# Layer 0 of a graph network on one core: where the gather loop waits for landings

## The chip, the cores and the metric

One Trainium2 chip, one of its NeuronCores. The time is the device time of one launch in microseconds (us); of three runs of the kernel before, the median is 8332.26 us (8326.56 to 8350.35). Engines are called PE (TensorE), DVE (VectorE), ACT (ScalarE), POOL (GpSimd) and SP (SyncE).

## The reference

There are 12,500 nodes of 16 features and 412,500 directed edges, sorted by destination. Each of two layers works on the normalised, rectified node features. The first layer is the one that matters here:

```
h = relu(edge_attr_16 @ W1 + b1)              # 256 values per edge
w_edge = (h @ W2 + b2).reshape(-1, 16, 16)    # a 16x16 matrix per edge
msgs = einsum('ei,eio->eo', x[src], w_edge)   # gathered source row times its matrix
aggr = segment_sum(msgs, dst)
out  = relu(batchnorm(aggr + x @ root + bias)); x = x + out
```

The second layer makes messages from `edge_attr_8` and again sums them by node. All is computed in float32, or in split parts that come to it.

## The kernel before

The kernel runs in stages, each with its own semaphores: `setup`, `layer0`, `between`, `layer1`, `finish`. The change is in `layer0` (L710 to L1155), which fills some 60 to 5036 us of the profiled execution.

`layer0` walks 404 groups of 1024 edges. A group is 128 partitions by T = 8 tiles. Every engine runs the same list of groups through `each_ring`, a loop whose body is four groups (buffers `r` = 0 to 3), and all order between engines is by counting semaphores.

- SP loads the edge features `ea` of a group (L779), 64 KB, two buffers.
- POOL, function `gather` (L795 to L807), fetches the source rows. For each tile it issues one indirect DMA that reads 128 rows of 128 bytes from the HBM table `gather_rows` into `xg[r][:, t, :]`. The row numbers are in `idx[r]`. There are 8 such gathers for a group, and 7 when `r` is 3 (from the second lap on), where PE and DVE make the eighth tile from a table in SBUF (`gather_dense`, `pick_rows`): 3132 in all. Before a group POOL waits for `idx_ready` and for the group four earlier to be done with the buffer. Before gather t, from the third on, it waits until gather t-2 of the same group has landed, and then adds one to `gathers_begun`. No instruction waits for `gathers_begun`.
- ACT, `body` (L872): two pairs of relus (`relu`, L842, from PSUM `ps_h` to `hT`), the copy `eT` (L836), then `indices` (L817), which writes `idx` three groups ahead (`AHEAD` = 3), then the splitting of edge features and messages.
- PE, `body` (L950 on): `hidden` (L906, two products into `ps_h`), `edge_weights` (L920, 16 instructions for half a group into four banks `ps_w`), `hidden`, `edge_weights`, `turn` (L896, transposes the features of the group two ahead), `gather_dense` in one group of four (L948), and `scatter` (L934, the sum by destination of the group before). `hidden` is written again only when ACT has read it, and it reads `eT`.
- DVE: `unit` (L1003) multiplies a bank `ps_w` with two tiles of `xg`; this is where a gathered row is first needed. `sum_unit` (L1010) adds up, `add_bias` (L1016) ends with `msg_ready`. Then follow the one-hot matrices (L1034) and the split of the messages.

After the last group's load SP also clears the tables that the second layer adds into (L595, L596).

Of the kernel before, what the change touches and what calls it, by code (L numbers as in the profile page):

```python
# [28 lines left out]
T = 8  # L29
# [22 lines left out]
def need(engine, sem, count):  # L52

    if isinstance(count, int) and count <= 0:
        return
    engine.wait_ge(sem, count)  # L56
# [15 lines left out]
def each_ring(engine, count, body, ring=4, laps=1):  # L72


    for c in range(laps * ring):
        body(c, c % ring, c // ring)
    assert count % ring == 0
    with engine.Fori(0, count // ring - laps - 1) as i:
        for u in range(ring):
            body(i * ring + (laps * ring + u), u, i + laps)  # L80
    for u in range(ring):
        c = count - ring + u
        body(c, u, c // ring)
# [626 lines left out]
def layer0(nc, S, k, sem, c, ea16, n_passes):  # L710
# [44 lines left out]
    xg_in = [[sem(f"xg_in{r}{t}") for t in range(T)] for r in range(RING)]  # L755
# [5 lines left out]
    def dense(r, lap):  # L761

        return r in DENSE and not (isinstance(lap, int) and lap == 0)
# [6 lines left out]
    with nc.Fori(0, n_passes) as _:  # L770
        with nc.Block() as block:

            @block.sync
            def _(sp):
                def load(g, r, lap):
                    s = r % 2
                    e0 = min(g * GE, S.E - GE) if isinstance(g, int) else sp.snap(g * GE)
                    need(sp, q["ea_used"], g - 1)
                    sp.dma_start(ea[s][:, :, :].rearrange("p t f -> p (t f)"),  # L779
                                 ea16[bass.ds(e0, GE), :].rearrange("(p t) f -> p (t f)", t=T)  # L780
                                 ).then_inc(ea_in[s], 16)
                    if dense(r, lap):
                        need(sp, q["col_free"], lap - 1)
                        sp.dma_start(col_b[:, :], k.col_rows[bass.ds(g, 1), :].broadcast_to([KP, P])
                                     ).then_inc(q["col_in"], 16)
                    if isinstance(g, int) and g == 1:
                        sp.dma_start(rows_in[:, :, :],
                                     k.rows[0:S.N, :].rearrange("(k p r) f -> p k (r f)", p=KP, r=KR)
                                     ).then_inc(q["node_in"], 16)
                each_ring(sp, G, load, RING, 2)  # L790
                clear_tables(sp, S, k, q["zeroed"])

            @block.gpsimd
            def _(pool):
                def gather(g, r, use):  # L795
                    pool.wait_ge(q["idx_ready"], g + 1)
                    need(pool, q["msg_ready"], g - RING + 1)
                    pool.sem_inc(q["gathers_begun"], 1)
                    for t in range(T - 1 if dense(r, use) else T):
                        if t >= 2:  # L800
                            pool.wait_ge(xg_in[r][t - 2], 16 * (use + 1))
                            pool.sem_inc(q["gathers_begun"], 1)
                        pool.indirect_dma_start(  # L803
                            xg[r][:, t, :], None, k.rows,
                            bass.IndirectOffsetOnAxis(ap=idx[r][:, t:t + 1], axis=0)
                        ).then_inc(xg_in[r][t], 16)
                each_ring(pool, G, gather, RING)  # L807

                pool.wait_ge(q["msg_ready"], G)
                pool.dma_reset()  # L810
# [1206 lines left out]
```

## Time and profile before

| what | us |
|---|---|
| median of three runs | 8332.26 |
| the profiled execution | 8296.17 |
| its span, first to last instruction | 8294.4 |
| `layer0`, from the first gather to the start of the next stage, about | 4976 |
| one group of it, 4976 / 404 | 12.3 |

The profiled execution is one run with the hardware profiler on; its span leaves out what lies before the first and after the last instruction, 1.8 us. A busy share over the whole span mixes the stages, which have different limits. "Idle before" is the time in which an engine did nothing ahead of an instruction, put down to the semaphore event that came last; "issue" means that no such event was seen just before, and "remote" that a semaphore moved for which the profile shows no source close enough in time. Ends of PE's instructions are modelled.

### The profile page before, as it was taken

The page shows a single profiled execution, that of the slowest core. Times are in us where ns is not written, and L with a number is a line of the kernel's source. Part 1 is how long each engine was busy: PE and PEld are TensorE (multiplying, and loading weights), DVE is VectorE, ACT ScalarE, POOL GpSimd, SP SyncE. Part 2 cuts the span into 40 slices and gives each one's busy share as a digit, 9 for nine tenths or more (in the row PEclk, how much of TensorE's full clock was granted, in tenths as well). Part 3 has the DMA queues.
Part 4 walks back from the last instruction along what each step waited for, and adds up shares of the span by engine and source line. Part 5 has one row for each costly group of instructions (what it writes and reads, how often), then busy time and mean ns, then how long its engine had stood idle before and what let it go on. Part 6 is the DMA issues. An engine that isn't in the chain of part 4 may idle for free. (4 is left out here: it accounts for less than half of the span.)

```text
span 8294.4 us, 193483 instructions
## 1 busy us (share of the span) xinstructions
PE 7333.8 (88%) x52997; PEld 6345.0 (76%) x52997; DVE 6680.6 (81%) x17449; ACT 4443.1 (54%) x8279; POOL 5653.6 (68%) x4866
## 2 busy tenths in 40 slices
PE   6888887888888888888888886999999999999998
PEld 5666666666666666666666665999999999999996
DVE  6667776777677777777777767999999999999997
ACT  4333343333333333333333434888888877778884
POOL 5656665666566666665666664888888888888886
PEclk8999999999999999999999998999999999999999
DMA  2111111111111111111111114445555555555544
GB/s 59 17 17 17 17 17 16 17 17 17 17 17 17 17 17 17 17 17 17 17 17 17 17 17 100 75 73 75 75 73 75 73 73 73 72 73 74 75 73 65
DMA packets 713464, 341.73 MB, mean 41 GB/s; under 512 B 422115, under 2 KB 656599, under 8 KB 713427
## 3 DMA queue, kind: packets, MB, share of 16 engines
q0 software_dynamic: 332928, 64.86, 13.5%
q1 hardware_dynamic: 379313, 272.94, 13.3%
q10 hardware_dynamic: 1186, 3.51, 0.1%
q8 instruction: 15, 0.25, 0.0%
q14 instruction: 22, 0.18, 0.0%
HBM read 307.85 MB, written 32.96 MB: 41 GB/s over the span
## 5 line engine op out<-in xcount | busy, mean ns | idle before, releaser
L803 POOL DMA_INDIRECT xg<-gather_rows,idx x3132 | 3001.6, 958 | 1996.5 <-issue 1259.3
L920 PE MATMUL ps_w<-W2s,hT 128*128 128x256 f32 x12928 | 3244.2, 406 | 63.0 <-issue 33.9
L920 PEld LDWEIGHTS ps_w<-W2s,hT 128*128 128x128 f32 x12928 | 2632.5, 205 | 627.7 <-issue 126.7
L1746 POOL DMA_INDIRECT sums<-total,row x1616 | 2548.8, 1577 | 541.8 <-issue 487.7
L1709 PE MATMUL ps_wide<-hot_col,placed 128*128 128x392 f32 x12928 | 2436.4, 345 | 9.1 <-DVE placed L1545 3.2
L1709 PEld LDWEIGHTS ps_wide<-hot_col,placed 128*128 128x128 f32 x12928 | 2315.3, 196 | 19.1 <-issue 12.8
L842 ACT ACTIVATE hT<-ps_h,b1c 128x512 f32<-128x512 f32 x1616 | 1024.7, 680 | 2288.5 <-remote 1662.2
L1003 DVE TENSOR_TENSOR prod<-ps_w,xg 128x512 f32<-128x512 f32 x1616 | 1082.2, 689 | 326.2 <-issue 66.1
L906 PE MATMUL ps_h<-eT,W1p 96*128 96x512 bf16 x1616 | 526.8, 407 | 656.3 <-ACT eT L836 480.1
L1644 ACT ACTIVATE square<-iota_col,minus_col 128x784 bf16<-128x784 int16 x1212 | 1061.2, 938 | 74.1 <-issue 57.6
L1545 DVE SCALAR_TENSOR_TENSOR placed<-ps_r,src_r,halves 128x512 fp32r<-128x512 f32 x1616 | 1099.1, 746 | 0.1
L1010 DVE TENSOR_REDUCE msg<-prod 128x32 f32<-128x512 f32 x1616 | 1059.6, 677 | 0.0
L1650 ACT ACTIVATE hot_col<-square,ones 128x2352 fp32r<-128x2352 bf16 x404 | 910.5, 2254 | 0.0
L1034 DVE TENSOR_SCALAR hot<-iota,rel_t 128x256 bf16<-128x256 bf16 x3232 | 737.8, 303 | 116.0 <-DVE ea_res L983 80.8
L983 DVE TENSOR_TENSOR ea_res<-ea,ea_parts 128x128 f32<-128x128 f32 x404 | 117.7, 291 | 858.3 <-ACT ea_parts L823 512.2
L906 PEld LDWEIGHTS ps_h<-eT,W1p 96*128 96x128 bf16 x1616 | 137.0, 97 | 811.5 <-issue 769.9
L1683 PE MATMUL ps_q<-q_win,hotT 128*128 128x128 bf16 x9696 | 609.6, 219 | 18.7 <-DVE hotT L1484 18.7
L1502 DVE TENSOR_TENSOR prod<-ps_q,e 128x512 f32<-128x512 f32 x808 | 553.9, 686 | 42.9 <-issue 40.8
L1683 PEld LDWEIGHTS ps_q<-q_win,hotT 128*128 128x128 bf16 x9696 | 548.1, 98 | 19.8 <-DVE hotT L1484 19.8
L1511 DVE TENSOR_REDUCE pre<-prod 128x64 f32<-128x512 f32 x808 | 550.7, 682 | 0.1
L852 ACT ACTIVATE parts<-msg_res 128x128 bf16<-128x128 f32 x404 | 125.0, 309 | 592.9 <-DVE msg_res L1022 428.9
L836 ACT ACTIVATE eT<-ps_e 96x1024 bf16<-96x1024 bf16 x404 | 408.9, 1012 | 1.9 <-PE ps_e L896 1.9
(229 smaller groups left out, 5613.6 us busy)
## 6 DMA issues: line engine op xcount, KB each, us to landing
dst_row<-dst_rows SPq DMA_DIRECT2D x404, 256.0 KB
src_row<-src_rows SPq DMA_DIRECT2D x404, 128.0 KB
xg<-gather_rows,idx POOLq DMA_INDIRECT x3132, 2.4
q_win<-q_rows SPq DMA_DIRECT2D x404, 96.0 KB
ea<-in_edge_attr SPq DMA_DIRECT2D x404, 64.0 KB
sums<-total,row POOLq DMA_INDIRECT x1616
e<-in_edge_attr SPq DMA_DIRECT2D x404, 32.0 KB
q_rows<-Q SPq DMA_DIRECT2D x12, 768.0 KB, 5.1
```

Source lines behind the costliest of these rows:

```text
L803: pool.indirect_dma_start(xg[r][:, t, :], None, k.rows, bass.IndirectOffsetOnAxis(ap=idx[r][:, t:t + 1], axis=0)).then_inc(xg_in[r][t], 16)
L842: a.activation(hT[s][:, j, :], ps_h[j][:, :], ACT.Relu, bias=k.b1[:, j:j + 1]).then_inc(q["relued"], 1)
L920: last = pe.matmul(to, hT[half][:, j, col:col + P], k.W2[:, j, :], start=(j == 0), stop=(j == 1 and not with_b2))
L1003: v.tensor_tensor(prod[u % 2][:, :, :, :], ps_w[u][:, :, :, :], xg[r][:, 2 * u:2 * u + 2, 0:D].unsqueeze(2).broadcast_to([P, 2, D, D]), AL ...
L1010: v.tensor_reduce(msg[s][:, 2 * u:2 * u + 2, :], prod[u % 2][:, :, :, :], X, ALU.add).then_inc(q["reduced0"], 1)
L1034: last = v.tensor_scalar(hot[s][:, t, :], k.iota[:, :], k.rel[:, bass.ds(g, 1), t:t + 1].rearrange("p g t -> p (g t)"), None, ALU.is_equal)
L1545: last = v.scalar_tensor_tensor(placed[s][:, w, :, :, :].rearrange("p r f a -> p r (f a)"), ps_r[:, :, :], src_r[:, bass.ds(g, 1), w], hal ...
L1644: last = a.activation(square[:, n, :], iota_col[:, :], ACT.Square, bias=minus_col[:, bass.ds(g, 1), WIDE - ACT_TILES + n])
L1650: a.activation(hot_col[s][:, WIDE - ACT_TILES:, :, :].rearrange("p w a b -> p (w a b)"), square[:, :, :].rearrange("p w b -> p (w b)"), AC ...
L1683: last = pe.matmul(ps_q[u][:, w, :, :].rearrange("p h j -> p (h j)"), hotT[s][:, t * P:(t + 1) * P], q_win[s][:, part * P:(part + 1) * P], ...
L1709: last = pe.matmul(ps_wide[:, 2 * r + a, 0:S.LC], placed[s][:, w, r * HR:(r + 1) * HR, :, part].rearrange("p r f -> p (r f)"), hot_col[s][ ...
L1746: pool.indirect_dma_start(k.sums[t], bass.IndirectOffsetOnAxis(ap=row[r][:, t:t + 1], axis=0), total[r][:, t, :], None, compute_op=ALU.add ...
```

## The change

POOL's wait for a landing stands in front of one gather of a group only. The fifth gather (t = 4) waits for the landing of the second (t = 1). The third, fourth, sixth, seventh and eighth are issued without a wait. `gathers_begun` is raised twice for a group and not seven times. What each gather fetches, the buffers, their number and all waits of the other engines stay.

```diff
                     pool.sem_inc(q["gathers_begun"], 1)
                     for t in range(T - 1 if dense(r, use) else T):
-                        if t >= 2:
-                            pool.wait_ge(xg_in[r][t - 2], 16 * (use + 1))
+                        if t == T // 2:
+                            pool.wait_ge(xg_in[r][t - 3], 16 * (use + 1))
                             pool.sem_inc(q["gathers_begun"], 1)
                         pool.indirect_dma_start(
                             xg[r][:, t, :], None, k.rows,
```

## Rows read from the trace of the kernel before

**Rows 1.** the page: busy time of each engine over the span

```profile
PE 7333.8 (88%) x52997; PEld 6345.0 (76%) x52997; DVE 6680.6 (81%) x17449; ACT 4443.1 (54%) x8279; POOL 5653.6 (68%) x4866
```

**Rows 2.** busy time by stretch; columns: stretch, us, then each engine

```profile
60.00:5036.00 4976.00, 4158.91 (x25124) 3305.26 (x25124) 3565.38 (x9890) 1914.77 (x4039) 3000.57 (x3132) 0.93 0.11 18
95.00:285.00 190.00, 159.17 (x972) 125.69 (x969) 137.69 (x382) 76.42 (x157) 117.01 (x122) 0.95 0.11 18
4986.00:5010.00 24.00, 20.36 (x139) 16.06 (x138) 18.43 (x52) 10.67 (x23) 6.83 (x8) 1.00 0.36 123
5036.00:8000.00 2964.00, 2890.95 (x25879) 2800.78 (x25880) 2834.26 (x6925) 2336.81 (x3860) 2415.22 (x1542) 0.99 0.52 76
```

**Rows 3.** groups of the first layer, 60 to 5036 us: busy, mean ns, idle before

```profile
L803 POOL DMA_INDIRECT xg<-gather_rows,idx x3132 | 3001.6, 958 | 1996.5 <-issue 1259.3 <-DMA xg<-gather_rows,idx 621.1 <-ACT idx L817 115.2
...
L1003 DVE TENSOR_TENSOR prod<-ps_w,xg 128x512 f32<-128x512 f32 x1612 | 1079.6, 689 | 325.9 <-issue 66.1 <-remote 54.8 <-DMA xg<-gather_rows,idx 38.0
...
L842 ACT ACTIVATE hT<-ps_h,b1c 128x512 f32<-128x512 f32 x1616 | 1024.7, 680 | 2288.5 <-remote 1662.2 <-PE ps_h L906 486.8 <-issue 135.4
...
L906 PE MATMUL ps_h<-eT,W1p 96*128 96x512 bf16 x1616 | 526.8, 407 | 656.3 <-ACT eT L836 480.1 <-issue 166.5 <-ACT hT L842 7.2
```

**Rows 4.** timeline of POOL, 2499 to 2507 us: start, length, [idle before]

```profile
2500.12 0.94 POOL L803 DMA_INDIRECT xg<-gather_rows,idx  x1 [0.30 <-issue]
2501.37 0.94 POOL L803 DMA_INDIRECT xg<-gather_rows,idx  x1 [0.30 <-issue]
2503.27 0.94 POOL L803 DMA_INDIRECT xg<-gather_rows,idx  x1 [0.96 <-DMA xg<-gather_rows,idx]
2504.52 0.94 POOL L803 DMA_INDIRECT xg<-gather_rows,idx  x1 [0.30 <-issue]
2506.48 0.94 POOL L803 DMA_INDIRECT xg<-gather_rows,idx  x1 [1.01 <-issue]
```

**Rows 5.** DMA issues of the page: median us from issue to landing

```profile
xg<-gather_rows,idx POOLq DMA_INDIRECT x3132, 2.4
```

**Rows 6.** instructions on tile xg, start to 2500 us: how many of each

```profile
L803 POOL DMA_INDIRECT xg<-gather_rows,idx x1536: 938/943/3520, 61.9 to 2498.7; - x192
L1003 DVE TENSOR_TENSOR prod<-ps_w,xg x784: 678/692/693, 82.7 to 2494.6; 128x512 f32<-128x512 f32 x196
```

**Rows 7.** waits, 95 to 285 us: us in total, times, longest

```profile
DVE prod L1003 <- DMA xg<-gather_rows,idx: 36.7, 27, 2.2
```

**Rows 8.** timeline of PE, 2500 to 2531 us, the hidden products

```profile
2500.47 0.59 PE L906 MATMUL ps_h<-eT,W1p 96*128 96x512 bf16 x2
...
2514.94 0.59 PE L906 MATMUL ps_h<-eT,W1p 96*128 96x512 bf16 x2
...
2530.15 0.59 PE L906 MATMUL ps_h<-eT,W1p 96*128 96x512 bf16 x2
```

**Rows 9.** timeline of ACT, 2506 to 2531 us: the relus of those products

```profile
2506.30 1.26 ACT L842 ACTIVATE hT<-ps_h,b1c 128x512 f32<-128x512 f32 x2 [6.06 <-remote]
...
2520.01 1.26 ACT L842 ACTIVATE hT<-ps_h,b1c 128x512 f32<-128x512 f32 x2 [7.40 <-remote]
...
2530.96 0.69 ACT L842 ACTIVATE hT<-ps_h,b1c 128x512 f32<-128x512 f32 x1 [4.78 <-PE ps_h L906]
```

**Rows 10.** timeline of all engines, 4986 to 5000 us

```profile
4998.12 1.08 POOL L803 DMA_INDIRECT xg<-gather_rows,idx  x1 [3.47 <-DMA xg<-gather_rows,idx]
...
4999.32 0.59 PE L906 MATMUL ps_h<-eT,W1p 96*128 96x512 bf16 x2
4999.80 0.69 ACT L842 ACTIVATE hT<-ps_h,b1c 128x512 f32<-128x512 f32 x1 [0.80 <-PE ps_h L906]
```

**Rows 11.** timeline of ACT and POOL, 2472 to 2476 us

```profile
2472.05 1.26 ACT L842 ACTIVATE hT<-ps_h,b1c 128x512 f32<-128x512 f32 x2 [8.74 <-remote]
...
2474.11 0.21 ACT L817 ACTIVATE idx<-src_t 128x8 int32 x1
...
2475.17 0.94 POOL L803 DMA_INDIRECT xg<-gather_rows,idx  x1 [1.90 <-ACT idx L817]
```

## The prediction

> **What bounds the kernel now.** I read the page's first part, then busy time by stretch, because the stages differ. Over the span PE is busy 88%, DVE 81%, POOL 68% [rows 1], which names no bound. By stretch, the first layer runs from 60 to 5036 us with PE at 4159 of 4976 us, and after 5036 us PE is at 2891 of 2964 [rows 2]. The change touches the first layer alone: 4976 / 404 groups = 12.3 us a group. PE needs 4159 / 404 = 10.3 us of that, DVE 8.8, ACT 4.7. So 2.0 us a group are nobody's work on PE, and I looked for what PE waits for.
>
> The groups of the stage show POOL's gather busy for 3002 us and idle for 1997 us before it, together 4998, that is the whole stage [rows 3]. A single pair of gathers shows why: starts at 2500.12, 2501.37, 2503.27, 2504.52, 2506.48. A gather takes 0.94 us, the next one starts 0.30 us later if nothing holds it, and every second one starts about 1.0 us later because it waits for a landing [rows 4]; a gather lands 2.4 us after its issue [rows 5]. A pair costs 3.15 us and a group of 7.75 gathers 12.2 us. POOL's own pace is thus nearly the pace of the stage, which would make it the bound if its users were waiting for it.
>
> They are not. By 2500 us POOL has issued 1536 gathers and DVE has begun 784 multiplications [rows 6]: at 7.75 gathers and 4 multiplications a group that is 198 groups against 196. POOL is about two groups ahead, and three is all that `AHEAD` allows. In the whole stage DVE's multiplication was let go by a gather's landing for 38.0 us, and by a source that the profile can't name for 54.8 us [rows 3]. Of the 38.0 us 36.7 fall between 95 and 285 us [rows 7], where 122 gathers in 190 us [rows 2] are 12.1 us a group: there POOL is the bound, in the first 17 groups or so. Later it isn't.
>
> The large wait is another: ACT's relu `hT` has 2289 us idle before it, 5.7 us a group, 1662 of them "remote", and PE's next hidden product then waits 656 us for what ACT makes after that relu [rows 3]. I followed three of these waits. The hidden products start at 2500.47, 2514.94 and 2530.15 [rows 8], and the relus that read them at 2506.30, 2520.01 and 2530.96 [rows 9]: 5.8, 5.1 and 0.8 us later, for two products that take 0.6. ACT has nothing else to do in these gaps. So PE's result reaches ACT late and irregularly, and PE, which can't go two halves further, stops. What was going on meanwhile? In the first case POOL issues two gathers with 0.30 us between (2500.12, 2501.37), then pairs, and the relu comes in the pause before 2506.48, 1.78 us after the start of the gather at 2504.52. At 4998 us the clearing of the tables slows the landings, POOL's gathers stand 3.5 us apart, and the relu follows 0.48 us after the start of its product [rows 10]. In that stretch the granted clock is 1.00 and the layer's is 0.93 [rows 2]. My reading is that PE's results get through late while gathers are in preparation one after another, and promptly in a pause of POOL. It rests on a few events and is not shown.
>
> The Trainium skill, page "Perfetto Trace Analysis", section on the Tensor Engine instruction, says that PE's end in a profile is estimated and that the semaphore moves only when PSUM has acknowledged all bytes. So PE's rows can't show the delay, and I measured from the start of PE's instruction to the start of its reader.
>
> **The change part by part.**
>
> 1. Removed: five of six waits in a group of 8 and four of five in a group of 7. Each second one now costs about 0.65 us (1.0 against 0.30 idle); those between are met already and cost nothing [rows 4]. Three a group, 1.9 us of POOL's time, go. The events on `gathers_begun` go with them; nobody waits for these.
> 2. The remaining wait. The fifth gather would start at 4 x 1.25 = 5.0 us, the second lands at 1.25 + 2.4 = 3.65 us. It is met, so at no cost; if more gathers in flight slow the landing, it bites only from 3.0 us on, and then by one pause a group.
> 3. POOL's new pace. 7.75 gathers at 0.96 + 0.30 = 1.26 us are 9.8 us a group (12.2 now). No gather waits on POOL behind another's landing. But the stage needs 12.3 us a group for reasons that lie elsewhere, so POOL now runs into its own wait for `idx`: eight gathers back to back, then a pause of some 2.5 us. It does this already at times [rows 11].
> 4. The direct gain. What DVE waited for gathers is at most 38.0 + 54.8 = 93 us in the stage, and it is gained only where nothing else is late. In the first 17 groups POOL is no longer the bound, but 12.1 us there turn into the 12.3 us of the rest. I take nothing, and keep -93 us as the bound.
> 5. The indirect effect, through the pattern of pauses. Now there is a pause of a microsecond every 3.15 us; afterwards one long pause a group. If results get through only in pauses, the loop closes like this: relu at 2472.05, `idx` done at 2474.32 (2.27 us), first gather at 2475.17 (0.85 us) [rows 11], start of the last of eight 8.75 us later (7.5 with seven), relu 1.78 us after that start. That is 13.65 us for three groups and 12.40 us for the fourth, mean 13.3, or 1.0 us above 12.3. Over the 387 groups behind the first 17 it is +395 us, the upper end. The lower end, if the results no longer meet a gather at the wrong moment, is PE's own 10.3 us: -2.0 x 404 = -810 us. Between ends so far apart I go by the nearest row: the relu at 2520.01 came 0.12 us after a gather that had started with 0.30 us idle before it, so results do get through inside a close pair, only more seldom. I take two fifths of 1.0 us: +0.4 x 387 = +155 us.
>
> Nothing else moves: SP's loads, the clearing of the tables, ACT's order and the second layer are as before. At the end of the stage the slow landings (3.5 us apart) are waited for less, but DVE's lack is in the 93 us above.
>
> The profiled execution is 8296.2 us, 36 below the median of 8332.3. By its own time the sum is 8296 + 155 = 8451; against the median it is 8332 + 155 = **8487 us**, and this is the forecast.
>
> **The rivals.**
>
> - *No change.* POOL is two groups ahead, and what it does with its slack meets nobody. For it: DVE's small waits. Against it: the relus' delays, for which the engines offer no other cause. Time: 8332, within 25 us.
> The Trainium skill, page "SBUF — State Buffer", section "SBUF: two separate sides", says that only DVE and GpSimd share a port and that PE and ACT never wait for anyone there. By that rule gathers can't hold up PE and this rival holds; the prompt relu at 4999.80 speaks against the rule, but doesn't refute it.
> - *Faster.* The delays hang on the chain of landings: a result gets through at certain points of POOL's cycle, and a shorter cycle brings these sooner. For it: the stage's 12.3 us are within 1% of POOL's own 12.2, which is odd for two things without a link, and in the first 17 groups, with POOL the bound, DVE waits 36.7 us in some 15.7 groups, so that its side could have run at 9.8 us there. Against: POOL rarely limits anyone later. Half of the way from 12.3 to PE's 10.3 is -1.0 x 404 = -404 us: 7930. With the direct waits alone it is 8240.
> - *Slower through missing pauses*, the forecast: place, the relu `hT` of each group; price up to 1.0 us; it decides from the point where the delay behind eight close gathers exceeds what the long pause gives back.
> - *The change doesn't do what it says*: landings slow from 2.4 to over 3.0 us with three in flight, and the one wait bites. POOL still gains two pauses of three. This stays inside the others.
>
> **How the numbers follow.** Slower 0.43, with 8360 to 8730 as its own range (0.1 to 1.0 us a group). No change 0.22. Faster 0.35, from 7530 (all of PE's 2.0 us) to 8300. A difference under 0.3% (25 us) can't be told from none. The range that leaves 2 in 10 out cuts the far part of the faster case and the end of the slower: 7950 to 8750.
>
> **What would show it.** Right in every case: POOL's idle before a gather falls to 0.30 us but for one long wait a group, put down to `idx` (115 us now [rows 3]), and POOL's busy time stays at 3000 us. The forecast: ACT's idle before `hT` grows from 2289 us towards 2440, the granted clock falls below 0.93, the stage ends near 5190 us. No change: these stay. Faster: the idle shrinks, and PE's wait for `eT` with it. The forecast is wrong if the relus follow their products more promptly with gathers close together, or if gathers themselves grow longer than 0.96 us.

## The result: slower in the timing of record, faster in two later jobs

In the timing of record, beside the kernel before, the changed kernel takes **9200.0 us** (median of 4 executions, 9192.9 to 9206.8) against 8337.6 (4 executions). The ratio is **1.103**, 95% interval 1.101 to 1.105. I forecast 8487: the right sign, a fifth of the size.

That isn't the whole result. Each job below ran on one chip, with the kernel before beside it; the chip of the timing of record has no number. In two later jobs, on two chips (8 and 9), the same changed kernel took 7302.2 and 7302.5 us, ratios **0.898** (0.897 to 0.900) and **0.897** (0.895 to 0.898). So the section first reads the slower outcome, and the experiments then tell the two apart. One of the ten executions of e13 took 17316 us, against 8126 to 8132 for the other nine, and is left out.

The page and the stretches of the changed kernel, answering to [rows 1, 2]. In a stretch the columns are its length, then PE, PEld, DVE, ACT and POOL busy, granted clock, DMA share, GB/s:

```profile
PE 7815.5 (85%) x52997; PEld 6547.4 (71%) x52997; DVE 6714.9 (73%) x17449; ACT 4424.4 (48%) x8279; POOL 5631.3 (61%) x4866
```

```profile
60.00:5930.00 5870.00, 4637.64 (x25077) 3502.33 (x25078) 3585.98 (x9867) 1893.75 (x4036) 2976.49 (x3132) 0.87 0.08 15
...
6000.00:8500.00 2500.00, 2469.31 (x22228) 2403.03 (x22227) 2407.42 (x5911) 1993.54 (x3294) 2067.62 (x1313) 0.99 0.52 76
```

The first layer now ends at 5930 us instead of 5036 [rows 2], which is the whole loss: 5870 / 404 = 14.5 us a group for 12.3. POOL's busy time is nearly the same (2976 us for 3001), PE's has grown by 479 us at a lower granted clock (0.87 for 0.93), and the instructions are as many. The groups, answering to [rows 3]:

```profile
L803 POOL DMA_INDIRECT xg<-gather_rows,idx x3132 | 2976.5, 950 | 2909.5 <-ACT idx L817 1991.0
...
L920 PE MATMUL ps_w<-W2s,hT 128*128 128x256 f32 x12928 | 3755.9, 436 | 833.5 <-issue 821.9
...
L842 ACT ACTIVATE hT<-ps_h,b1c 128x512 f32<-128x512 f32 x1616 | 1018.4, 680 | 3324.5 <-remote 2850.1
...
L1003 DVE TENSOR_TENSOR prod<-ps_w,xg 128x512 f32<-128x512 f32 x1616 | 1079.4, 689 | 924.7 <-remote 694.2
```

POOL has one long wait a group, for `idx`: 385 of them, 1991 us. The relu `hT` waits 3325 us instead of 2289 [rows 3]. Grown is the idle time of PE's edge-weight matmuls, 822 us by "issue", with nothing that PE would wait for; in the kernel before it was 34:

```profile
L920 PE MATMUL ps_w<-W2s,hT 128*128 128x256 f32 x12928 | 3244.2, 406 | 63.0 <-issue 33.9
```

The timeline of the changed kernel shows what that is (start, length, [idle before]):

```profile
3011.16 0.95 POOL L803 DMA_INDIRECT xg<-gather_rows,idx  x1 [0.30 <-issue]
...
3012.41 0.94 POOL L803 DMA_INDIRECT xg<-gather_rows,idx  x1 [0.30 <-issue]
3013.66 0.94 POOL L803 DMA_INDIRECT xg<-gather_rows,idx  x1 [0.30 <-issue]
3014.03 0.19 PEld L920 LDWEIGHTS ps_w<-W2s,hT 128*128 128x128 f32 x1 [0.80 <-issue]
3014.73 0.38 PE L920 MATMUL ps_w<-W2s,hT 128*128 128x256 f32 x1 [1.04 <-issue]
3014.76 0.19 PEld L920 LDWEIGHTS ps_w<-W2s,hT 128*128 128x128 f32 x1 [0.54 <-issue]
3015.45 0.38 PE L920 MATMUL ps_w<-W2s,hT 128*128 128x256 f32 x1 [0.34 <-issue]
3016.15 1.38 PEld L920 LDWEIGHTS ps_w<-W2s,hT 128*128 128x128 f32 x7 [1.21 <-issue]
3016.15 1.77 PE L920 MATMUL ps_w<-W2s,hT 128*128 128x256 f32 x7 [0.33 <-issue]
3016.41 1.26 ACT L842 ACTIVATE hT<-ps_h,b1c 128x512 f32<-128x512 f32 x2 [7.07 <-remote]
...
3019.53 0.94 POOL L803 DMA_INDIRECT xg<-gather_rows,idx  x1 [4.92 <-ACT idx L817]
```

Late in a burst of eight gathers PE still works, but its instructions start some 0.7 us apart; about 1.5 us after the last gather's end it runs at full pace again, and the late relu comes with it. It is so in most groups: by my means over the middle of the layer the edge-weight matmuls start 0.23 to 0.31 us apart in the first 5 us of a burst, and 0.63 to 0.86 us apart from 7 to 11 us after its start. From there the loop is closed: relu, `idx`, next burst.

### The profile page after: what moved, and what is told of

Same layout as the page of the kernel before. It is cut to its first block and busy times, and to the rows that moved or that the text cites. A ratio compares the mean times of both kernels' runs of the same rounds, so it can differ in the third digit from the quotient of the medians.

```text
span 9191.2 us, 191563 instructions
## 1 busy us (share of the span) xinstructions
PE 7815.5 (85%) x52997; PEld 6547.4 (71%) x52997; DVE 6714.9 (73%) x17449; ACT 4424.4 (48%) x8279; POOL 5631.3 (61%) x4866
## 3 DMA queue, kind: packets, MB, share of 16 engines
q1 hardware_dynamic: 379313, 272.94, 11.8%
## 5 line engine op out<-in xcount | busy, mean ns | idle before, releaser
L920 PE MATMUL ps_w<-W2s,hT 128*128 128x256 f32 x12928 | 3755.9, 436 | 833.5 <-issue 821.9
L920 PEld LDWEIGHTS ps_w<-W2s,hT 128*128 128x128 f32 x12928 | 2823.1, 220 | 1743.1 <-issue 1245.2
L1034 DVE TENSOR_SCALAR hot<-iota,rel_t 128x256 bf16<-128x256 bf16 x3232 | 783.7, 324 | 115.9 <-DVE ea_res L983 113.9
```

The lines of the kernel that those rows point to most:

```text
L920: last = pe.matmul(to, hT[half][:, j, col:col + P], k.W2[:, j, :], start=(j == 0), stop=(j == 1 and not with_b2))
L1034: last = v.tensor_scalar(hot[s][:, t, :], k.iota[:, :], k.rel[:, bass.ds(g, 1), t:t + 1].rearrange("p g t -> p (g t)"), None, ALU.is_equal)
```

## Experiments

Eighteen runs in five jobs. The jobs of e1 to e8 (the kernel before: 8157 and 8303 us) ran on chip 1. The jobs of e9 to e18 (8158, 8130, 8143 us) ran on chips 2, 9 and 8. All of the first came before all of the second.

A relu is late when ACT waits for it long after PE's product has begun. I take the mean time from the start of the product to the start of the relu, over the relus before which ACT was idle, and call it the delay. It is 3.6 us in the kernel before, 4.5 in the changed one, and 0.4 to 0.5 in each trace of e9 to e18. The time of the kernel before doesn't tell the two cases apart: 8157 us stands beside a late e1, 8158 beside a prompt e9. Ratios are to the kernel before of the same job; us a group is my mean over the middle four fifths of the layer.

**First job.**

e1 keeps the events and drops only the waits:

```
 if t == T // 2: pool.wait_ge(xg_in[r][t - 3], 16 * (use + 1))
+if t >= 2: pool.sem_inc(q["gathers_begun"], 1)
```

> The changed kernel's single wait, but the event on gathers_begun stays in front of every gather from the third on. Theory C (closeness: eight gathers back to back hold up PE, and only a real pause of about 0.65 us between pairs lets it run): the events cost POOL some 0.05 us each and make no pause, so 9200 us within 60. Rival E (the extra instruction on POOL's queue, not the pause, is what matters): about 8340 us.

9132.1 us, ratio 1.119 (1.117 to 1.121), with a delay of 4.2 us; the time is 8 us below the expected range. The idle time between two close gathers is 0.305 us with an event and without one (the median in e1 and in the changed kernel), so the events are free and cover nothing. Rival E falls.

e2 makes the pauses without waiting for a landing:

```
-if t >= 2: pool.wait_ge(xg_in[r][t - 2], ...)
+if t in (2, 4, 6): pool.memset(pause[:, :], 0.0)   # 1 x 640, and a wait for its end
```

> No wait for a landing at all; in front of the third, fifth and seventh gather POOL clears a small buffer of its own (640 numbers of one partition, an estimated 0.65 us, from 514 ns for 512). Theory C: the pauses are back, whoever makes them, so 8340 us within 100. Rival L (what matters is how many gathers are in flight, or that a landing is awaited): as changed, 9200 us within 100.

8664.8 us, ratio 1.062 (1.061 to 1.064): outside both expectations. The pause came out at 1.40 us, so POOL's pace became 13.2 us a group. The waits of the layer up to 4200 us (us in total, times, longest) say what this means:

```profile
DVE prod L1005 <- DMA xg<-gather_rows,idx: 1051.8, 570, 4.4
ACT hT L844 <- PE ps_h L908: 722.3, 267, 5.5
```

The late relus are nearly gone (2.6 us of "remote" in this stretch, a delay of 0.84 us), and DVE now waits for gathers: POOL's pace is the bound. Three pauses of 1.40 us a group cure the lateness though no landing is awaited, but they cost more than they cured.

e3 leaves the gathers out:

```
-pool.indirect_dma_start(xg[r][:, t, :], ...)        # and DVE's waits on xg_in
+v.memset(tile, 0.5) for each xg, once
```

> The first layer without its gathers: the gathered rows are a constant 0.5 set once, POOL only waits for idx and msg_ready, DVE waits for no landing. Everything else, ACT's idx included, stays. Theory C and any theory by which gathers hold PE up: 10.3 to 10.6 us a group instead of 12.3 (before) and 14.5 (changed), so 4180 to 4300 us of first layer and 7500 to 7650 us in all; the relus follow their products by under 1 us. Rival S (the schedule of PE, ACT and DVE itself makes the 12.3): 12 us a group or more, about 8250 us.

7265.6 us, ratio 0.891 (0.889 to 0.892), 9.7 us a group, and so below the range of 10.3 to 10.6: PE's 10.3 us was no floor, as its busy time itself falls to 9.4 us a group (3783 us of 3920 up to 3980 us) at a granted clock of 1.00 for 0.93. Here the relus wait only for PE, with a delay of 0.42 us:

```profile
L836 ACT ACTIVATE hT<-ps_h,b1c 128x512 f32<-128x512 f32 x1612 | 1014.7, 680 | 684.3 <-PE ps_h L900 683.8
```

So 684 us of idle before `hT` is the schedule's own, and the gathers add the rest. The rival, that the schedule itself needs 12.3, falls.

e4 moves the burst in PE's cycle (no landing waits):

```
+need(pool, q["scattered"], g - 3)       # before a group's gathers
 indices(g + AHEAD, ...)                 # ACT: now ahead of the relus
```

> No landing waits, but the burst of a group's gathers is moved to another place in PE's cycle: ACT makes idx ahead of its relus, and POOL begins the burst for group n only when PE has finished the scatter of group n - 4. Theory C with a place (a burst hurts through PE's 48 short instructions of turn and scatter, which then fall behind it): the burst ends at 8.7 of PE's 10.3 us, turn and scatter lie in the pause, and the layer takes 10.5 to 11.5 us a group, 7650 to 8000 us in all. Theory C without a place (a burst costs PE the same wherever it lies): 14 to 14.5 us a group, 9000 to 9200 us.

8244.9 us, ratio 1.011 (1.009 to 1.012), 12.2 us a group. Neither expectation holds, but nine tenths of the loss of e1 are gone with bursts just as long. Where a burst lies matters. The waits up to 4200 us:

```profile
ACT hT L840 <- PE ps_h L904: 1813.6, 353, 8.3
PE ps_a L932 <- issue: 471.4, 604, 1.9
```

The delay is 0.67 us (e1: 4.2), and the edge-weight matmuls start 0.22 to 0.29 us apart through the whole burst. But PE stops in the scatter (`ps_a`), which now meets the end of the burst, for no reason that the profile names. The next product begins late, and ACT is idle before `hT` for 2318 us over the layer, against 3273 in e1 and 689 in e3. The burst still costs PE time, at another place and less of it.

**Second job.** After the first I formed theory D, that a group needs some 4.8 us outside the gathers.

e5 is e4's gate with the landing waits of the kernel before kept.

> The kernel before with its waits for landings, and with the burst moved as in e4_gate (idx made ahead of the relus; POOL begins group n when the scatter of n - 4 is done). Theory D (duty: PE's instructions get through only in the time in which POOL is not inside a gather, so a group costs POOL's 7.36 us in gathers plus about 4.8 us outside them, wherever these lie): 12.2 us a group, 8150 us within 60. Rival C with a place (pauses between pairs and a good place add up): 11.5 us a group or less, 7900 us or less.

8250.7 us, ratio 0.994 (0.992 to 0.995), 12.1 us a group. The figure per group fits D; the time is 40 us above its range, in a job in which the kernel before was 146 us above the first job's. The gate gains 0.6% here, and the relus are as late as before (delay 3.5 us).

e6 is e2 with a buffer of 32 numbers.

> As e2_filler, no landing waits, but the buffer that POOL clears in front of the third, fifth and seventh gather is 32 numbers instead of 640, so a pause of some 0.85 us instead of 1.40 (and 1.0 in the kernel before). POOL's pace becomes about 11.9 us a group. Theory D: 12.2 us a group, 8150 us within 80: the pauses are in pairs as before, whoever makes them. Rival L (the landing that is awaited matters, as the pause then ends when a DMA is done): 8600 us or more.

8388.9 us, ratio 1.011 (1.009 to 1.013), 12.5 us a group. Late relus are back (1518 us of "remote" up to 4200 us, e2: 2.6; delay 3.8 us, e2: 0.84). Pauses of about 0.9 us (0.12 of clearing, 0.78 around it) don't prevent them, those of 1.40 do; but e2 also made POOL the bound, at 13.2 us a group for 12.5, and the length of the pause isn't told apart from that. Neither expectation holds: rival L's 8600 us isn't reached, and D is 0.3 us a group and 159 us above its range.

e7 gathers six tiles a group:

```
-for t in range(T - 1 if dense(r, use) else T):
+for t in range(T - 2):                   # the last two tiles stay 0.5
```

> The kernel before with its waits, but each group gathers six tiles instead of 7.75 (the last two tiles keep a constant 0.5). Theory D: 6 x 0.95 + 4.8 = 10.5 us a group, 7480 us within 100. Rival C (pairs are as close as before, so PE is held up as much): between 11.5 and 12.2 us a group, 7900 to 8150 us.

7479.4 us, ratio 0.900 (0.899 to 0.902): D's 7480 is met, with 10.3 us a group for its 10.5. The relus are still late, by 2.2 us.

e8 loads as many bytes through SyncE's queue:

```
+sp.dma_start(xg[r][:, t, :], k.rows[t * P:t * P + P, :]).then_inc(xg_in[r][t], 16)
```

> The same 7.75 tiles of 128 x 32 numbers a group, with the same semaphores for their landings, but loaded as plain slices of the table by SyncE's queue, one after another, with no gather on POOL (what is loaded is rows 0 to 1023, not the indexed rows). Theories C and D (POOL's gathers are what holds PE up): as e3_no_gathers, 9.7 to 9.9 us a group, 7270 to 7370 us. Rival M (the transfers into SBUF or their landings hold PE up, whoever issues them): near 12 us a group, 8100 us.

7314.3 us, ratio 0.881 (0.879 to 0.883), 677 us of idle before the relus and a delay of 0.42 us, as in e3. Plain transfers of as many bytes, with as many landings, do no harm; POOL's gathers do. Rival M falls. What e8 doesn't tell apart is POOL's work on a gather from the indexed form of the transfer, since it left out both.

**Third job.**

e9 makes the change's one wait bite:

```
 if t == T // 2:
-    pool.wait_ge(xg_in[r][t - 3], 16 * (use + 1))
+    pool.wait_ge(xg_in[r][t - 1], 16 * (use + 1))
```

> The change with a wait that is not met: the fifth gather waits for the fourth (issued 3.75 us after the group's first, landing 2.4 us later), so one pause of some 1.4 us in the middle of eight gathers, and POOL's pace becomes about 10.9 us a group. Theory D (7.36 us in gathers plus at least 4.7 us outside, and time outside counts only while PE can still take something): between the kernel before and the changed one and nearer to before, 12.3 to 13.2 us a group, 8330 to 8700 us. Rival C (only bursts of two are short enough, any longer one stops PE): as changed, 9100 us.

8080.2 us, ratio 0.991 (0.989 to 0.993), 11.8 us a group. Both expectations fail, on the good side. POOL goes in bursts of eight (four of one group, four of the next) with 2.3 us between them, and no relu is late (delay 0.46 us). The second view is of the layer up to 4200 us:

```profile
2506.67 0.94 POOL L803 DMA_INDIRECT xg<-gather_rows,idx  x1 [0.31 <-issue]
2509.92 0.94 POOL L803 DMA_INDIRECT xg<-gather_rows,idx  x1 [2.31 <-DMA xg<-gather_rows,idx]
2511.16 0.95 POOL L803 DMA_INDIRECT xg<-gather_rows,idx  x1 [0.30 <-issue]
```

```profile
ACT hT L842 <- PE ps_h L906: 723.9, 349, 5.2
DVE prod L1003 <- DMA xg<-gather_rows,idx: 706.4, 573, 3.7
```

e10 adds e4's gate to it.

> e4_gate with that one real wait in the middle of the group: two bursts of four, the first right behind PE's scatter, a pause of 1.4 us, the second, and a pause until the next scatter. Theory D: 12.0 to 12.1 us a group, ratio to before 0.985 to 0.995. If the place of a burst mattered by itself: 11.5 us or less, ratio 0.96.

8082.5 us, ratio 0.991 (0.990 to 0.993). The number fits D, the reason doesn't: it equals e9, and DVE waits 715 us for gathers up to 4200 us. The bound is POOL's pace, and a gate can't help.

e11 and e12 put an event in front of each of PE's 32 edge-weight matmuls, with and without gathers:

```
+pe.sem_inc(q["spare"], 1)
 last = pe.matmul(to, hT[half][:, j, col:col + P], k.W2[:, j, :], ...)
```

> The kernel before with one more instruction in front of each of PE's 32 edge-weight matmuls of a group: an event on a semaphore that nobody reads. To be read against e12_pe_events_no_gathers, which has the same events without gathers. Theory I (what gets through only outside the gathers is PE's supply of instructions, so more instructions need more time outside): the slowdown against its kernel without events is clearly larger here than there, by 0.5 us a group (200 us) or more. Rival N (it is the delivery of PE's results, whatever the count of instructions): the slowdown is no larger here than there.

> e3_no_gathers (first layer without gathers, rows a constant 0.5) with the same event in front of each of PE's 32 edge-weight matmuls. It prices the events where no gather disturbs: 0 to 1.0 us a group above the 9.7 of e3_no_gathers, 7265 to 7670 us.

8155.2 us, ratio 1.000 (0.999 to 1.001), and 7245.3 us, 20 us below its range and ratio 0.889. The events cost nothing that shows in either. It looked like a verdict against theory I, but e11 has no late relus at all, so there was nothing to lengthen: inconclusive.

**Fourth job.** That made me suspect the chip, and I ran both kernels again, on a third one.

> The kernel before, unchanged, with a profile from the same chip as its neighbours here. Its time has come out at two levels, 8146 to 8168 us and 8297 to 8350 us. If the late relus (5 us and more behind their products) are a property of the kernel, its trace shows ACT idle before hT of some 1900 to 2300 us in the layer at either level; if they belong to the upper level alone, it shows under 1000 us at the lower one.

8129.4 us, and idle before `hT` of 830 us, where the first trace had 2289 [rows 3]. This stretch is 60 to 4890 us:

```profile
L803 POOL DMA_INDIRECT xg<-gather_rows,idx x3131 | 2978.6, 951 | 1871.8 <-DMA xg<-gather_rows,idx 1142.2 <-issue 695.9 <-ACT idx L817 33.7
...
L1003 DVE TENSOR_TENSOR prod<-ps_w,xg 128x512 f32<-128x512 f32 x1612 | 1078.3, 689 | 1057.6 <-DMA xg<-gather_rows,idx 829.7 <-PE ps_w L920 84.3 <-issue 56.2
...
L842 ACT ACTIVATE hT<-ps_h,b1c 128x512 f32<-128x512 f32 x1616 | 1017.2, 680 | 830.0 <-PE ps_h L906 829.6
```

The late relus are not a property of the kernel alone. Without them the same code is bound by POOL's gathers: DVE waits 830 us for them, not 38, and POOL's own pauses wait for landings (1142 us) and hardly for `idx` (34 us).

> The changed kernel, unchanged, on the same chip as its neighbours. 1.10 to 1.12 of the kernel before, 9000 to 9200 us.

7302.2 us, ratio 0.898 (0.897 to 0.900). The expectation fails: the time is 1700 us below its range. The changed kernel's page and its layer from 60 to 4000 us:

```profile
L803 POOL DMA_INDIRECT xg<-gather_rows,idx x3132 | 3024.6, 966 | 1002.3 <-issue 849.0
...
L842 ACT ACTIVATE hT<-ps_h,b1c 128x512 f32<-128x512 f32 x1616 | 1017.2, 680 | 683.2 <-PE ps_h L906 682.8
L1003 DVE TENSOR_TENSOR prod<-ps_w,xg 128x512 f32<-128x512 f32 x1616 | 1079.7, 689 | 233.0 <-issue 59.6
```

```profile
60.00:4000.00 3940.00, 3773.19 (x24732) 3027.65 (x24733) 3474.00 (x9727) 1907.53 (x3984) 2979.26 (x3087) 1.00 0.12 22
```

Gathers with 0.30 us between them for the whole layer, PE at 3773 of 3940 us, clock 1.00, and the relus as prompt as without gathers (e3: 684 us). The last gather starts at 4066 us, against 4891 in e13.

e15 waits for the third landing (`xg_in[r][t - 2]`), e16 replaces the wait by a buffer of 1500 numbers cleared at `t == T // 2`.

> Between the changed kernel (the fifth gather waits for the second, a wait that is met) and e9_real_wait (for the fourth, a pause of 2.3 us): here it waits for the third, issued at 2.50 us, landing 2.4 us later at 4.9, against its turn at 5.0: barely a pause, under 1 us. Theory P (a group needs one pause that is long enough to clear what eight gathers have piled up): little is won, 8700 to 9200 us. Rival W (any wait that bites is enough): 8080 to 8200 us.

> No wait for a landing; in front of the fifth gather POOL clears a buffer of 1500 numbers of one partition (an estimated 1.5 us, with 0.78 around it), so one pause of 2.3 us a group as in e9_real_wait, but timed. Theory P and theory D (time outside the gathers counts, whoever makes it): 8080 to 8180 us. Rival L (the gather must be held until a landing has come): 8500 us or more.

7558.3 us, ratio 0.930 (0.929 to 0.932), and 8028.8 us, ratio 0.988 (0.986 to 0.989). e15 is below all expectations; e16 is 51 us below the range of P and D, and they don't explain it. In these traces the time goes with POOL's pauses (idle over 0.35 us between gathers, my sum per group):

```
kernel            pauses, us   us a group   us        ratio
changed (e14)     0.06          9.87        7302.2    0.898
e15               0.98         10.50        7558.3    0.930
e16               2.25         11.69        8028.8    0.988
e9 (third job)    2.42         11.81        8080.2    0.991
before (e13)      3.33         11.89        8129.4    1.000
```

About 7.4 us in gathers, 0.30 us for each close gap and the pauses add up to each line, as they must; that POOL sets the pace is seen from what is waited for, landings by POOL and gathers by DVE (e13): for the kernel before 7.37 + 3.86 x 0.30 + 3.33 = 11.86; for the changed one 7.47 + 7.7 x 0.30 + 0.06 = 9.84, which is also about e3's 9.7. Theories P and D, that a group needs time outside the gathers, are false here: the changed kernel has 2.40 us of it.

**Fifth job**, the changed kernel and e9's on one more chip.

> The changed kernel once more, as it came out at 1.103 of the kernel before (9200 us) where it was first timed and at 0.898 (7302 us) on another chip. Theory K (two conditions of a chip: in one a relu follows its product by microseconds while gathers are close, in the other never): one of the two ratios again, 1.10 to 1.12 with ACT's idle before hT over 2500 us, or 0.89 to 0.91 with it under 1000 us, and nothing between. Rival G (a gradual difference between chips): something between, 0.92 to 1.08.

> The kernel of e9_real_wait (the fifth gather waits for the fourth) on the same chip as e17_changed_third. If the relus are prompt here: 0.991 of the kernel before again, as POOL's pace sets the time. If they are late here: theory P (the pause of 2.3 us clears what eight gathers have piled up) 0.98 to 1.01; rival A (a late condition hits every burst of eight) 1.04 or more.

7302.5 us, ratio 0.897 (0.895 to 0.898), and 8075.5 us, ratio 0.992 (0.991 to 0.994). Idle before `hT` is 685 us in the changed kernel. Theory K's two outcomes are what came, with nothing between. But that it is the chip isn't shown: no chip was seen in both conditions, chip 1 wasn't timed again, and all late jobs came before all prompt ones, so that a condition that ended in time fits as well. Where relus are prompt no kernel with all its gathers beats the changed one. No job of the late kind came again, so e9's kernel was never timed there: whether it is good in both is open.

## Why the prediction was right in sign and wrong in size

- **Steps 1 and 2, the waits that go and the one that stays.** Right. In e13 and e14 POOL's pauses fall from 3.33 to 0.06 us a group; the kept wait costs nothing. That the events cover nothing is e1's.
- **Step 3, POOL runs into `idx`.** Right in the timing of record: 385 waits, though of 5.2 us each (1991 / 385) and not of 2.5, as the stage grew to 14.5 us a group. On chips 8 and 9 POOL's 9.8 us a group is right, and the long wait doesn't come, as the rest then keeps up.
- **Step 5, the loop of the burst.** This is the step that failed. Its upper end was relu to first gather 3.12 us, burst 8.75, last gather's start to relu 1.78, mean 13.3 us a group. Measured in the changed trace (my means over its groups): 3.20, 8.54 (both sorts of group) and 2.82, together 14.56, the period itself. So the loop was the right one, and closed in nearly every group, and the measured time lies above what I had called its upper end. Two sizes were off. The last term is 2.82, not 1.78: that is 1.0 us. I had read it from one burst of the kernel before, made of pairs, in which PE doesn't crawl as it does late in eight close gathers. And I took two fifths of the loop's cost on one relu that came between close gathers, which gave away another 0.6. With the forecast's 0.4 us a group these make 2.0 of the measured 2.2; the first two terms, larger by 0.1 each, are the rest.
- **Step 4, the direct gain of nothing, at most 93 us.** Nothing contradicts it where the relus are late, since POOL's lack hides behind them. On chip 9 it is 827 us (8129 to 7302), the whole result. The trace before me held a hint: in the first 17 groups DVE did wait for gathers [rows 7], and 12.3 us of stage beside 12.2 us of POOL was "odd for two things without a link".
- **The rivals.** "Faster" named that coincidence, and chips 8 and 9 went its way, further than its 7930 us; its mechanism (results get through at points of POOL's cycle) was not theirs. "No change" rested on POOL's slack, and neither outcome bears it out. As to the rule of the Trainium skill's page "SBUF — State Buffer", section "SBUF: two separate sides": PE is not held up by POOL's gathers on two chips (e14, e17), and is on chip 1 (e1 against e3), by a way that needn't be a port. So the rule agrees with the traces of those two chips, and no trace here refutes it as a rule of ports; as a reason for "no change" it failed.
- **The signs, in the timing of record.** POOL's gaps and busy time came as told. Idle before `hT` went to 3325 us, not 2440; the clock to 0.87; the end of the stage to 5930, not 5190.

What is shown: POOL's gathers, not the bytes, landings or events, hold up PE and the relus in one condition (e1, e3, e8); longer pauses make the relus prompt (e2), and short ones or another place of the burst take away most of the loss of e1 and not the cause (e4, e6); in the other condition the same gathers hold up nobody (e14, e17). What is not: what the condition is.

The late traces have one mark in common. In the kernel before a third of the records of PE's, ACT's and DVE's semaphore updates are missing by my count (0.63 to 0.67 present in each stretch of 250 us; 0.56 to 0.80 in the changed kernel and in e1, e2 and e4 to e7), in each trace of e9 to e18 one in a hundred at most. Of the 50,112 landing events of the gathers 18,138 are recorded in the kernel before and 10,682 in the changed one, but 49,535 in e13. This too needs the gathers: on the same chip 1 nothing is missing in e3, and e8, with 50,112 landings by SyncE's queue, has all of them recorded. So the sheer number of landing records isn't what loses them. And lost records alone don't make relus late: e2 lacks a fifth to a quarter of its updates at a delay of 0.84 us. The Trainium skill, page "NOTIFIC — the notification-queue block", section "Overflow: three behaviours, one of which stalls the engine", says that the path that records events always holds back its producers inside the block, rather than losing a record there. That could join late engines to a crowded recording path, though it doesn't say why records are lost. No run here switched the recording off. Every execution of e1 to e18 has a granted clock of its own on record, so they may all have been recorded, and whether the kernels would be late without it is open. Theory I wasn't settled either.

## What to carry to other kernels

Before a trace's stalls go into a sum, ask whether they are the kernel's: waits that the profile calls "remote" and idle time on PE by "issue" called for a second trace from another chip. One like e13's, with 830 us of gathers in DVE's way, might have turned this forecast round. Where an engine's own pace (12.2 us) is within a per cent of the stage's (12.3), treat it as the bound until an experiment without it says otherwise. And a change whose sign hangs on such a condition is timed on several chips before it is kept or dropped.

## What the runs showed of the hardware

- The same program on the same inputs took 9200 us in one timing and 7302 us on each of two chips later, repeatable within 0.2% each time, while the medians of the kernel before lay between 8129 and 8338 us.
- In the late condition PE starts its edge-weight matmuls 0.63 to 0.86 us apart late in a burst of eight gathers 1.25 us apart (changed kernel), and 0.22 to 0.29 us apart when the burst lies elsewhere in its cycle (e4). Pauses of 1.40 us between pairs bring the relus' delay down to 0.84 us (e2); with pauses of about 0.9 us it is 3.8 us (e6).
- As many plain loads through SyncE's queue on chip 1 do neither: delay 0.42 us, no record missing (e8).
- 32 more events a group on PE cost nothing (7245 against 7266 us without gathers, on different chips; 8155 against 8158 us with them, on chip 2, where POOL is the bound).
